# Mask copies ahead of the expert weights, and the second expert weights in 112 and 6 rows

## The chip, the cores and the metric

The kernel runs on one core of a Trainium2 chip. The metric is the device time of one execution in microseconds. It computes two transformer blocks in float32 for 8 batch rows of 100 tokens of 512 channels, with 361 context tokens.

## The reference

What is computed, cut to its outline (layer norms, softmax and quantisations are written out in full in the reference):

```
x = x + state_mix(layernorm(x), ctx)          # linear recurrence over ctx, its mean added, norm
x = x + bitlinear_ffn(layernorm(x))           # 512 -> 2048 -> 512, ternary weights, gelu
q = w8a8(layernorm(x), wq); k = ctx @ wk.T + bk; v = ctx @ wv.T + bv
s = q @ k.T / sqrt(32) + mask                 # 16 heads, mask of 100 x 361 per batch row
x = x + w8a8(softmax(s) @ v, wo)
g, e = top2(layernorm(x) @ gate.T + bias)     # 8 experts
x = x + sum(g * (silu(z @ w1[e].T + b1[e]) @ w2[e].T + b2[e]))
```

## The kernel before

The kernel is written engine by engine, with semaphores between them. There are three stages.

Stage A (to about 295 us) makes keys into `CT` (one slice per batch row) and values into `VS` (read as `vs(b)`) for all 8 batch rows, and runs the first attention and the feed-forward layer.

Stage B (from about 296 us, its loop from 340 us) is the attention, one batch row b at a time, 16 heads in 4 groups. TensorE (PE) makes the scores of a group, four heads at once (`scores`, L786), and runs one group ahead: the first scores of batch b + 1 are made within batch b. VectorE (DVE) adds the mask, takes the row minimum and writes `sN` (L1164, reading `maskS`), ScalarE takes the exponential (L598), PE turns the probabilities (L794) and multiplies them by the values (L807, `mix_group`). Between heads DVE also prepares the rows of batch b + 1 and finishes those of batch b - 1; GpSimd scales the queries that the next batch's first scores need. Having passed all heads of batch b, DVE makes a small copy (L1172) that raises `mask_used`.

`maskS` has two slots, and batch b uses slot b % 2. The masks of batches 0 and 1 are loaded in front of the loop (L310). The mask of batch b + 2 may be loaded once batch b is through, and DVE waits for it (`mask_in0`, `mask_in1`) when batch b + 2 begins.

SyncE (SP) issues all copies of this stage in program order, in `expert_loads(b, j, more)` (L313 to 320). When all scores of batch b are made, the keys of batch b are used up, and the first weights of expert b go into their place (L315, 704 KB, 128 rows). When all of batch b is mixed (semaphore `mixed`), its values are used up too, and the second weights of expert b go there (L317, 708 KB, 118 rows of 1536 floats). After it stands the wait for `mask_used` and the mask copy (L320, 141 KB, 100 rows of 361 floats). Batches 6 and 7 have `more` false, thus no mask to load.

Stage C (from about 556 us) routes the tokens to the experts. SP loads the router's weights and biases (L329 to L331, 16, 3.1 and 3.1 KB) and `b1B`, the first biases of all experts spread to 128 rows (L332, 1408 KB), and DVE waits for these four before its first instruction of the stage (L1191). PE waits for `experts_in`, the count of all expert copies, 16 for each copy. From 629 us on, 20 blocks of 128 rows run through the experts, bound by PE.

Of the kernel before, what the change touches and what calls it, by code (L numbers as in the profile page):

```python
# [14 lines left out]
B, S, D = 8, 100, 512  # L15
T = 361
# [11 lines left out]
WP = D * FF // P // NW  # L28
E, EH = 8, 352
EC = 118  # L30
EHP = 3 * EC
TOPK = 2
NBLK = (B * S * TOPK + E * (P - 1)) // P
# [7 lines left out]
def block_kernel(nc, x, ctxT, mask, decay, win, b_in, wout, b_out, gamma0, beta0, w1, w2, gammaf,  # L41
                 wq, bq, wk, bk, wv, bv, wo, bo, gate_w, gate_b, gate_bias, ew1, eb1, ew2, out):
    with ExitStack() as whole:  # L43
        def sb(stack, name, shape, dt=F32):
            return stack.enter_context(nc.sbuf_tensor(name, shape, dt))
# [3 lines left out]
        def sem(name):  # L49
            if name not in sems:  # L50
                sems[name] = whole.enter_context(nc.semaphore(name))
            return sems[name]
# [8 lines left out]
        def after(count):  # L61

            return count + 1
# [20 lines left out]
        def vs(b):  # L84
            return VS[:, bass.ds(b * (NT * VW), NT * VW)]
# [43 lines left out]
        maskS = sb(bb, "maskS", [P, 2, T + 1])  # L129
# [46 lines left out]
        share, backI = sb(cc, "share", [P, NBLK]), sb(cc, "backI", [P, NBLK], I32)  # L176
        hb, hs, hTe = sb(cc, "hb", [P, 2, EH]), sb(cc, "hs", [P, 2, EHP]), sb(cc, "hTe", [P, 2, 3, P])
        yb = sb(cc, "yb", [P, 2, D])
# [56 lines left out]
        def groups_mixed(groups):  # L235

            return groups + 2
# [7 lines left out]
        def read_by_heads(eng, b):  # L245

            for r in range(HPC):
                eng.wait_ge(sem(f"score{r}"), after((b + 1) * KC))
# [11 lines left out]
        def _(sp):  # L260
# [50 lines left out]

            def expert_loads(b, j, more):

                read_by_heads(sp, b)
                sp.dma_start(CT[:, b, 0:KC * EH], ew1[b]).then_inc(sem("experts_in"), 16)  # L315
                sp.wait_ge(sem("mixed"), groups_mixed((b + 1) * KC))
                sp.dma_start(vs(b)[0:EC, 0:3 * D], ew2[b]).then_inc(sem("experts_in"), 16)  # L317
                if more:
                    sp.wait_ge(sem("mask_used"), b + 1)
                    sp.dma_start(maskS[0:S, j, 0:T], mask[b + 2]).then_inc(sem(f"mask_in{j}"), 16)  # L320

            with sp.Fori(0, B // 2 - 1) as it:
                for j in range(2):
                    expert_loads(it * 2 + j, j, True)
            expert_loads(B - 2, 0, False)
            expert_loads(B - 1, 1, False)

            sp.wait_ge(sem("b_done"), 4)
# [24 lines left out]
        def _(g):  # L353
# [120 lines left out]
            for j in range(2):  # L474

                g.memset(hs[:, j, EH:EH + 1], 1.0).then_inc(sem("c_setup"), 1)
                g.memset(hs[:, j, EH + 1:EHP], 0.0).then_inc(sem("c_setup"), 1)
            g.iota(z[0:S, :, C_TOK:ZW], [[S, B], [0, ZW - C_TOK]], base=1, channel_multiplier=1,
# [25 lines left out]
        def _(act):  # L504
# [128 lines left out]
            def step(s, j, u):  # L633
                if started(s):
                    act.wait_ge(sem("h_turned"), s)
                    act.copy(hTe[0:EC, 1 - j].rearrange("p c s -> p (c s)"), ps[0:EC, 5 - j, 0:3 * P])\  # L636
                       .then_inc(sem("hT"), 1)
# [16 lines left out]
        def _(pe):  # L654
# [202 lines left out]
            pe.matmul(ps[:, 0, 0:1], ones[:, :], ones[:, 0:1], start=True, stop=True).then_inc(sem("b_done"), 1)  # L857

            pe.wait_ge(sem("b_done"), 4)
            pe.wait_ge(sem("experts_in"), 32 * E)  # L860
            pe.wait_ge(sem("c_in"), 64)

            for b in range(B + 1):
# [30 lines left out]
            def step(s, j, u):  # L894
# [7 lines left out]
                if started(s):  # L902
                    pe.wait_ge(sem("h_act"), s)
                    for c in range(3):
                        mm = pe.transpose(ps[0:EC, 5 - j, c * P:(c + 1) * P], hs[:, 1 - j, c * EC:(c + 1) * EC], ident[:, :])  # L905
                    mm.then_inc(sem("h_turned"), 1)
                if within(s, 1):
                    turn_x(s + 1, 1 - j, u + j)
                if started(s):
                    e = block_expert(mybir.EngineType.PE, s - 1)  # L910
                    pe.wait_ge(sem("hT"), s)
                    for c in range(3):
                        mm = pe.matmul(ps[:, 7 - j, :], hTe[0:EC, 1 - j, c, :], vs(e)[0:EC, c * D:(c + 1) * D],  # L913
                                       start=(c == 0), stop=(c == 2))
# [422 lines left out]
```

## Time and profile before

| | |
|---|---|
| runs | 773.19, 777.51, 779.58 us; median 777.51 |
| profiled execution | 778.72 us, its span 776.6 us |
| PE busy | 542.8 us, 70% |
| DVE busy | 365.1 us, 47% |
| ScalarE (ACT) busy | 296.9 us, 38% |
| GpSimd (POOL) busy | 179.6 us, 23% |
| DVE in stage B, waiting for scores | 51.0 us, 26 times |
| DVE in stage B, waiting for a mask | 18.8 us, 5 times |
| copies | 62.58 MB, mean 81 GB/s |

How to read it: the span is the time from the first to the last instruction in the profile; the execution's own time is 2.1 us more. A share of busy time is a mean over all stages. PEclk is the clock granted to TensorE as a part of 2.4 GHz; a full 1.00 or a 0.50 (1.2 GHz) stand in most short windows. The DMA share is the mean busy share of the core's 16 copy engines, so that two engines at work show as 0.12 or 0.13.

### The profile page before, as it was taken

The numbers are of one execution on the slowest core, as the hardware profiler recorded it, in microseconds if no ns is written. First come the engines' busy times: TensorE is split into PE (matmuls) and PEld (weight loads), VectorE is DVE, ScalarE is ACT, GpSimd is POOL, SyncE is SP. The second block draws the span as 40 slices with busy tenths as digits, with TensorE's granted clock in tenths as the row PEclk, the third lists the DMA queues.
The fourth block names the chain that finished last, engine by engine and source line by source line (L and its number), as shares of the span: only waits on it lengthen the run. The fifth ranks groups of instructions, "written<-read, shape, count | busy, mean of one in ns | idle before, by whom it ended". The sixth has DMA issues, their size and how long they took to land. (4 is left out here: it accounts for less than half of the span.)

```text
span 776.6 us, 10875 instructions
## 1 busy us (share of the span) xinstructions
PE 542.8 (70%) x3388; PEld 382.2 (49%) x3388; DVE 365.1 (47%) x962; ACT 296.9 (38%) x631; POOL 179.6 (23%) x211
## 2 busy tenths in 40 slices
PE   0062299999999993149967887769237049999991
PEld 0042277777777772126645655547137025555550
DVE  5646656676657663443655566644152112222210
ACT  4156333444343420435755666666011002222220
POOL 1001121332223220121323233421200611222221
PEclk9995589999999997555867688885655559999996
DMA  8959200000000003101212221212220434445544
GB/s 336 418 189 342 89 11 0 11 11 11 0 11 11 0 1 129 26 0 39 74 37 62 79 78 38 65 69 76 102 96 1 124 92 83 83 83 85 91 58 111
DMA packets 22915, 62.58 MB, mean 81 GB/s; under 512 B 3779, under 2 KB 9699, under 8 KB 20827
## 3 DMA queue, kind: packets, MB, share of 16 engines
q1 hardware_dynamic: 18462, 53.47, 20.1%
q0 software_dynamic: 4416, 8.63, 7.0%
q8 instruction: 22, 0.36, 0.2%
q14 instruction: 15, 0.11, 0.1%
HBM read 46.40 MB, written 17.32 MB: 82 GB/s over the span
## 5 line engine op out<-in xcount | busy, mean ns | idle before, releaser
L1164 DVE CUSTOM_DVE_ANT_0 sN<-ps,maskS 100x361 f32<-100x361 f32 x128 | 64.7, 532 | 79.8 <-PE ps L786 51.0
L794 PE MATMUL ps<-ident,pE 100*121 100x100 f32 x384 | 81.3, 349 | 8.1 <-ACT pT L589 8.0
L794 PEld LDWEIGHTS ps<-ident,pE 100*121 100x121 f32 x384 | 64.3, 241 | 43.3 <-issue 33.2
L598 ACT ACTIVATE pE<-sN,nmx 100x361 f32<-100x361 f32 x128 | 77.4, 605 | 21.2 <-DVE nmx L1164 21.2
L589 ACT COPY pT<-ps 121x300 f32<-121x300 f32 x128 | 51.3, 402 | 37.9 <-PE ps L794 37.8
L786 PE MATMUL ps<-CT,qn 32*100 32x361 f32 x256 | 39.9, 704 | 30.7 <-DVE nmx L1164 27.3
L913 PE MATMUL ps<-VS,hTe 118*128 x120 | 56.7, 609 | 5.5 <-ACT hTe L636 5.5
L499 POOL DMA_INDIRECT sums_out<-yb,backI x20 | 31.1, 1554 | 109.5 <-ACT yb L646 105.4
L899 PE MATMUL ps<-CT,xT 128*128 x160 | 53.3, 477 | 2.0 <-DVE xT L1257 2.0
L1271 DVE TENSOR_TENSOR hb<-ps,b1B 128x352 f32<-128x352 f32 x20 | 10.5, 525 | 88.7 <-PE ps L899 88.7
L899 PEld LDWEIGHTS ps<-CT,xT 128*128 128x128 f32 x160 | 31.3, 197 | 24.9 <-issue 12.8
L1046 DVE TENSOR_REDUCE tk<-h 100x1 f32<-100x512 f32 x32 | 20.0, 680 | 39.5 <-ACT h L549 39.4
L689 PE MATMUL ps<-cxH,wkH 128*128 128x364 f32 x128 | 31.1, 368 | 8.9 <-DVE cxL L984 4.5
L913 PEld LDWEIGHTS ps<-VS,hTe 118*128 118x128 f32 x120 | 21.1, 189 | 29.3 <-issue 29.3
L669 PE MATMUL ps<-kvw,w1s 128*128 128x8 f32 x32 | 7.0, 361 | 40.0 <-DMA y<-in_b_out 40.0
L891 PE MATMUL ps<-ident,xin 128*128 128x128 f32 x80 | 12.5, 281 | 30.2 <-DMA xin<-slots_in 30.2
L646 ACT ACTIVATE yb<-ps,share 128x512 f32<-128x512 f32 x20 | 13.7, 687 | 51.3 <-PE ps L913 51.3
L402 POOL TENSOR_SCALAR hq<-h 100x1024 bf16<-100x1024 f32 x8 | 10.3, 1290 | 93.8 <-DVE h L1053 93.8
L542 ACT ACTIVATE CT<-ps,biases 128x364 f32 (+1 forms) x32 | 17.9, 564 | 36.7 <-PE ps L689 35.8
L807 PE MATMUL ps<-pT,VS 121*32 121x100 f32 x768 | 30.5, 308 | 0.6 <-ACT pT L589 0.6
L786 PEld LDWEIGHTS ps<-CT,qn 32*100 32x100 f32 x256 | 11.6, 216 | 38.2 <-issue 31.1
L689 PEld LDWEIGHTS ps<-cxH,wkH 128*128 128x128 f32 x128 | 22.8, 206 | 14.3 <-issue 7.1
(233 smaller groups left out, 1141.7 us busy)
## 6 DMA issues: line engine op xcount, KB each, us to landing
VS<-in_w SPq DMA_DIRECT2D x8, 1024.0 KB, 9.2
CT<-in_ctxT SPq DMA_DIRECT2D x8, 728.0 KB, 16.8
VS<-in_ew SPq DMA_DIRECT2D x8, 708.0 KB
CT<-in_ew SPq DMA_DIRECT2D x8, 704.0 KB
slots_in<-zeros SPq DMA_DIRECT2D x5, 1056.0 KB, 12.4
xin<-slots_in SPq DMA_DIRECT2D x20, 264.0 KB, 3.4
XR<-in_x SPq DMA_DIRECT2D x1, 1600.0 KB
summB<-summary_rows SPq DMA_DIRECT2D x8, 200.0 KB
```

What stands on the lines that cost most here:

```text
L499: g.indirect_dma_start(sums_out, bass.IndirectOffsetOnAxis(backI[:, t:t + 1], 0), yb[:, t % 2, :], None, bounds_check=B * S + P - 1, compu ...
L542: act.activation(CT[:, b, m * TP:(m + 1) * TP], ps[:, m % 2, 0:TP], ACT.Identity, bias=biases[:, 1, m:m + 1]).then_inc(sem("k_copied"), 1)
L589: act.copy(pT[0:TC, ht % (2 * HPC)].rearrange("p c s -> p (c s)"), ps[0:TC, 4 + r, 0:NT * S])\
L598: act.activation(pE[0:S, q, 0:T], sN[0:S, q, 0:T], ACT.Exp, scale=-1.0, bias=nmx[0:S, h_:h_ + 1], accum_out=sums[0:S, j, h_:h_ + 1]).then_ ...
L689: mm = pe.matmul(ps[:, m % 2, 0:TP], wt[:, k, m * P:(m + 1) * P], cx[:, k, :], start=(n == 0), stop=(n == 3 * KC - 1))
L786: pe.matmul(ps[0:S, r, 0:T], qn[at, b % 2, g, :], CT[at, b, g * TP:g * TP + T], start=True, stop=True)\
L794: mm = pe.transpose(ps[0:TC, 4 + r, c * S:(c + 1) * S], pE[0:S, h_ % HPC, c * TC:(c + 1) * TC], ident[0:S, 0:S])
L807: mm = pe.matmul(ps[r * HD:(r + 1) * HD, 6, g * S:(g + 1) * S], vs(b)[0:TC, at:at + HD], pT[0:TC, (g * HPC + r) % (2 * HPC), c, :], start= ...
L899: mm = pe.matmul(ps[:, 2 + j, 0:EH], xT[:, j, k, :], CT[:, e, k * EH:(k + 1) * EH], start=(k == 0), stop=(k == KC - 1))
L913: mm = pe.matmul(ps[:, 7 - j, :], hTe[0:EC, 1 - j, c, :], vs(e)[0:EC, c * D:(c + 1) * D], start=(c == 0), stop=(c == 2))
L1046: ins = dve.tensor_reduce(tk[0:S, 14 + m:15 + m], h[0:S, m * 512:(m + 1) * 512], AX.X, ALU.max, apply_absolute_value=True)
L1164: dve.tensor_tensor_reduce(out=sN[0:S, q, 0:T], in0=ps[0:S, q, 0:T], in1=maskS[0:S, j, 0:T], scale=-1.0, scalar=3.4e38, op0=ALU.add, op1=A ...
```

## The change

The wait for `mask_used` and the mask copy go from the end of `expert_loads` to its beginning, ahead of the wait for the scores. The second weights go as two copies of 112 rows (`EVEN`, the largest multiple of 16 in 118) and 6 rows. Each raises `experts_in` by 16, so PE's wait at the start of stage C asks for 48 instead of 32 for each expert.

```diff
--- before.py
+++ after.py
@@ -28,6 +28,7 @@
 WP = D * FF // P // NW
 E, EH = 8, 352
 EC = 118
+EVEN = EC // 16 * 16
 EHP = 3 * EC
 TOPK = 2
 NBLK = (B * S * TOPK + E * (P - 1)) // P
@@ -311,13 +312,14 @@
 
             def expert_loads(b, j, more):
 
+                if more:
+                    sp.wait_ge(sem("mask_used"), b + 1)
+                    sp.dma_start(maskS[0:S, j, 0:T], mask[b + 2]).then_inc(sem(f"mask_in{j}"), 16)
                 read_by_heads(sp, b)
                 sp.dma_start(CT[:, b, 0:KC * EH], ew1[b]).then_inc(sem("experts_in"), 16)
                 sp.wait_ge(sem("mixed"), groups_mixed((b + 1) * KC))
-                sp.dma_start(vs(b)[0:EC, 0:3 * D], ew2[b]).then_inc(sem("experts_in"), 16)
-                if more:
-                    sp.wait_ge(sem("mask_used"), b + 1)
-                    sp.dma_start(maskS[0:S, j, 0:T], mask[b + 2]).then_inc(sem(f"mask_in{j}"), 16)
+                for rows in (slice(0, EVEN), slice(EVEN, EC)):
+                    sp.dma_start(vs(b)[rows, 0:3 * D], ew2[b, rows]).then_inc(sem("experts_in"), 16)
 
             with sp.Fori(0, B // 2 - 1) as it:
                 for j in range(2):
@@ -857,7 +859,7 @@
             pe.matmul(ps[:, 0, 0:1], ones[:, :], ones[:, 0:1], start=True, stop=True).then_inc(sem("b_done"), 1)
 
             pe.wait_ge(sem("b_done"), 4)
-            pe.wait_ge(sem("experts_in"), 32 * E)
+            pe.wait_ge(sem("experts_in"), 48 * E)
             pe.wait_ge(sem("c_in"), 64)
 
             for b in range(B + 1):
```

On SP, in the loop body of stage B, for one batch. Before, `CT<-in_ew` being the first and `VS<-in_ew` the second expert weights:

```order
L315 ISA [waits score2,score3,score1,score0]
L315 DMA CT<-in_ew 128x1408
L316 REGISTER_ALU
L317 ISA [waits mixed]
L317 DMA VS<-in_ew 118x1536
L320 ISA [waits mask_used]
L320 DMA maskS<-in_mask 100x361
```

and now (the row of L249 holds the wait for the scores):

```order
L317 ISA [waits mask_used]
L317 DMA maskS<-in_mask 100x361
L249 ISA
L319 ISA [waits score2,score3,score1,score0]
L319 DMA CT<-in_ew 128x1408
L320 REGISTER_ALU
L322 ISA [waits mixed]
L322 DMA VS<-in_ew 112x1536
L322 ISA
L322 DMA VS<-in_ew 6x1536
```

The mask copy has moved past both weights and both of their waits; the second weights are two copies.

On SP, from the last batch of B to the start of C. Before:

```order
L315 DMA CT<-in_ew 128x1408 [waits score2,score3,score1,score0]
L317 DMA VS<-in_ew 118x1536 [waits mixed]
L329 DMA gwT<-in_gate_w 128x32 [waits b_done]
L330 DMA gbB<-in_gate_b 100x8
L331 DMA gbB<-in_gate_bias 100x8
L332 DMA b1B<-in_eb 128x2816
```

and now:

```order
L319 DMA CT<-in_ew 128x1408 [waits score2,score3,score1,score0]
L322 DMA VS<-in_ew 112x1536 [waits mixed]
L322 DMA VS<-in_ew 6x1536
L331 DMA gwT<-in_gate_w 128x32 [waits b_done]
L332 DMA gbB<-in_gate_b 100x8
L333 DMA gbB<-in_gate_bias 100x8
L334 DMA b1B<-in_eb 128x2816
```

No mask stands here; only the second weights have become two copies, ahead of what stage C loads.

## Rows read from the trace of the kernel before

**Rows 1.** the page, part 1: busy time, share of the span, instructions

```profile
PE 542.8 (70%) x3388; PEld 382.2 (49%) x3388; DVE 365.1 (47%) x962; ACT 296.9 (38%) x631; POOL 179.6 (23%) x211
```

**Rows 2.** waits of DVE, 330 to 560 us: total, times, longest

```profile
DVE sN L1164 <- PE ps L786: 51.0, 26, 4.0
DVE sN L1164 <- DMA maskS<-in_mask: 18.8, 5, 5.0
```

**Rows 3.** timeline of DVE: start, us, line, tiles, [idle before <-releaser]

```profile
365.55 0.54 DVE L1164 CUSTOM_DVE_ANT_0 sN<-ps,maskS 100x361 f32<-100x361 f32 x1 [2.89 <-PE ps L786]
...
391.31 0.54 DVE L1164 CUSTOM_DVE_ANT_0 sN<-ps,maskS 100x361 f32<-100x361 f32 x1 [4.70 <-DMA maskS<-in_mask]
...
443.39 0.54 DVE L1164 CUSTOM_DVE_ANT_0 sN<-ps,maskS 100x361 f32<-100x361 f32 x1 [0.21 <-issue]
...
517.89 0.53 DVE L1164 CUSTOM_DVE_ANT_0 sN<-ps,maskS 100x361 f32<-100x361 f32 x1 [5.00 <-DMA maskS<-in_mask]
```

**Rows 4.** timeline of SP's copies, batch 0 to 1 of stage B

```profile
373.70 0.26 SPq L317 DMA_DIRECT2D VS<-in_ew  x1
374.17 0.29 SPq L320 DMA_DIRECT2D maskS<-in_mask  x1
```

**Rows 5.** windows of 1 us: length, busy time by engine, PEclk, DMA share, GB/s

```profile
384.00:385.00 1.00, 0.79 (x8) 0.53 (x6) 0.87 (x4) 0.85 (x2) 0.92 (x2) 1.00 0.98 393
388.00:389.00 1.00, 0.98 (x14) 0.79 (x6) 0.00 (x0) 0.48 (x3) 0.00 (x0) 1.00 0.12 49
392.00:393.00 1.00, 0.00 (x0) 0.00 (x0) 0.82 (x3) 0.95 (x3) 0.02 (x1) 0.54 0.03 8
```

**Rows 6.** windows of batches 0 to 7, first L1164 to L1172, columns as rows 5

```profile
340.59:362.51 21.92, 16.75 (x124) 11.72 (x125) 11.13 (x40) 11.62 (x37) 4.00 (x5) 0.50 0.06 16
365.55:386.47 20.92, 19.47 (x209) 13.85 (x208) 14.60 (x50) 15.54 (x50) 7.47 (x7) 0.77 0.19 64
391.31:413.95 22.64, 18.09 (x173) 12.28 (x173) 14.50 (x50) 14.45 (x46) 7.46 (x7) 0.70 0.21 64
417.68:443.04 25.36, 21.17 (x173) 14.59 (x173) 14.60 (x50) 14.44 (x46) 7.47 (x7) 0.60 0.20 63
443.39:465.14 21.75, 18.17 (x209) 12.63 (x207) 14.59 (x50) 15.71 (x52) 8.55 (x8) 0.84 0.23 70
467.21:488.74 21.53, 17.14 (x177) 11.38 (x176) 14.59 (x50) 14.33 (x46) 7.47 (x7) 0.84 0.22 67
492.49:512.75 20.26, 15.70 (x173) 10.76 (x173) 14.58 (x49) 14.33 (x46) 7.47 (x7) 0.83 0.19 67
517.89:536.64 18.75, 16.39 (x131) 11.21 (x131) 10.47 (x39) 11.64 (x37) 1.26 (x1) 0.51 0.15 52
```

**Rows 7.** copies by kind: KB each, us from issue to landing

```profile
wst<-in_wq SPq DMA_DIRECT2D x1, 1024.0 KB, 4.8
wst<-in_wo SPq DMA_DIRECT2D x1, 1024.0 KB, 6.9
```

**Rows 8.** timeline of PE, scores (L786), and of DVE at 447.53

```profile
385.80 0.87 PE L786 MATMUL ps<-CT,qn 32*100 32x361 f32 x8
...
394.41 1.54 PE L786 MATMUL ps<-CT,qn 32*100 32x361 f32 x8 [5.26 <-DVE nmx L1164]
...
446.49 0.87 PE L786 MATMUL ps<-CT,qn 32*100 32x361 f32 x8 [0.87 <-DVE nmx L1164]
447.53 0.54 DVE L1164 CUSTOM_DVE_ANT_0 sN<-ps,maskS 100x361 f32<-100x361 f32 x1 [1.18 <-PE ps L786]
...
512.09 0.87 PE L786 MATMUL ps<-CT,qn 32*100 32x361 f32 x8
```

**Rows 9.** timeline, end of B and start of C, SP and DVE

```profile
544.72 0.25 SPq L317 DMA_DIRECT2D VS<-in_ew  x1
...
557.44 0.35 SPq L332 DMA_DIRECT2D b1B<-in_eb  x1
...
565.49 0.69 DVE L1191 BATCH_NORM_STATS2 st6c<-XR 100x6 f32<-100x512 f32 x1 [9.71 <-DMA b1B<-in_eb]
```

## The prediction

> **What bounds the kernel now.** First the page's own totals [rows 1]: in a span of 776.6 us no engine is full, PE being busy for 70%, so the time is a sum of stages, each with its own last wait. The changed copies are issued in stage B (attention, from 340 us) and read in B (masks) and in stage C (experts). So I read who VectorE (DVE) waited for in B, and at the start of C [rows 2]. In B most of its idle time (51.0 us) ends on the scores from TensorE (PE), but 18.8 us, in five pieces, end on the copy of a mask. C begins with 9.7 us that end on a copy [rows 9].
>
> Next, where these five stand. DVE ends a batch with a small copy (L1172) and begins the next with the first L1164. The idle time ahead of that one tells [rows 3]: batch 2 begins after 4.70 us idle, batch 7 after 5.00 us, both for the mask (batches 3, 5 and 6 lie between, with 3.59, 1.93 and 3.60 us, all of the same kind). Batch 4 begins after 0.21 us, for nothing that the profile shows, and batch 1, whose mask is one of the two loaded in front of the loop, after 2.89 us, for the scores.
>
> Then why the mask is late [rows 4]: SP issues the second expert weights at 373.70 and the mask right behind, at 374.17; the mask is used at 391.31. That is 17.1 us for 141 KB. The windows say what the copy engines did in between [rows 5]: a share of 0.12 to 0.13 of 16 engines, or two engines, moving 49 GB/s, up to the moment the mask is in (392 to 393 us: 0.03). The first expert weights (704 KB) by contrast reach 0.98 and 393 GB/s. A 708 KB copy (725,000 bytes) at 50 GB/s takes 14.5 us, and what shares its two engines waits for it. So 118 rows go over two engines, and the mask's rows, whatever engines they are given, partly stand behind them.
>
> The Trainium skill, DMA: Bandwidth & Descriptors, section on why a DMA increments its semaphore by 16, says the number of engines is the largest up to 16 that divides the outer size of both sides: 118 gives 2, 112 gives 16, 6 gives 6, 100 gives 10. The share of 0.12 agrees for 118. The same page's rules for kernel authors speak against the second edit: two copies to disjoint partitions serialize on the same engines, so one should be used; by that the split is worth nothing and the sum below ends 1.5 us higher. The rule is written of copies that already use all 16, and the 0.12 of this trace is not that case.
>
> **The change part by part.** *Mask ahead of the weights (6 masks, batches 2 to 7).* Mask b+2 is now issued when batch b has ended: for batch 2 at 362.7 us instead of 374.17 (batch 0's window ends with its L1172 at 362.51 [rows 6]). It is needed at about 386.8. No such mask was seen travelling alone; the nearest row is a seven times larger copy that landed 4.8 us after issue [rows 7], and the farthest bound is the 17.1 us of today behind a slow copy. With either the mask is in by 380 us, 7 us before its need. All five stalls should go by this edit alone.
>
> What is late next at a batch's start: DVE's own L1172 and the scores. PE begins the scores of batch 2 at 385.80 and of batch 7 at 512.09, in both cases just before DVE is through [rows 8]; the three batches between are alike. From such a start at full clock to the first L1164 is 1.04 us (446.49 to 447.53). So batch 2 could begin at 386.84, 0.23 us after L1172's end (386.61, where its idle time of 4.70 begins), and batch 7 at 513.13, 0.24 us after. Batch 4 shows the same 0.21. Gain: 18.8 - 5 x 0.24 = 17.6 us. Bounds from the rows: all of it, 18.8; or, if each new batch waits for scores as batch 1 did at half clock (2.89 us), 4.70 + 3.59 + 3.60 + 5.00 - 4 x 2.89 = 5.3 us (batch 5 then gains nothing). I take 17.6, since these scores ran at full clock (0.87 us at 385.80 and at 512.09, against 1.54 us at 394.41, at half).
>
> Is the stall paid back within the batch? Batches 1 and 4 started without one and took 20.92 and 21.75 us; 2, 3, 5 and 6 started with one and took 22.64, 25.36, 21.53 and 20.26 [rows 6]. The starved ones are no faster, so nothing is given back.
>
> *The order on SP.* The wait for mask_used now stands ahead of the first expert weights, which so far went out at the batch's last scores. They are now issued when the batch has ended; nothing reads them before C, and the wait for "mixed" behind them opens later still (batch 0 ends at 362.51, its second weights go out at 373.70). Cost: 0. Batches 6 and 7 carry no mask and are not moved. The three queued items behind the new wait (weights 1, weights 2, next mask) serve nobody within this time.
>
> *112 and 6 rows.* Eight more copies of some 0.25 us on SP (the length of the old issue), which is idle: 0. For masks the split is cover, not gain. It pays at the end of B. The last second weights go out at 544.72 and, at 50 GB/s, hold two engines until about 560; b1B, the last copy that DVE needs for C, goes out at 557.44, and DVE starts C at 565.49 [rows 9]. With 16 engines the weights are in by about 549.5 (a copy of 1024 KB landed after 4.8 us), and b1B meets free engines. Bounds of the gain. From above: two 1024 KB copies issued 0.4 us apart landed 4.8 and 6.9 us after issue [rows 7], so a further 1024 KB costs 2.5 us; 1408 KB then need 2.3 + 3.5 = 5.8 us, landing at 563.3: gain 2.2 us. From below: by the bytes the old weights are done at 544.72 + 14.5 = 559.2 or soon after, and 14 of the 16 engines are free for b1B anyway, so memory may be its limit: 0. I take 1.5 us, nearer to the rows of whole copies, which are of the same kind.
>
> *The clock.* A stall of DVE becomes one of PE: behind batch 2's stall PE began the next scores at 394.41 after 5.26 us idle [rows 8], and the granted clock fell in 392 to 393 us (mean 0.54 of 2.4 GHz, thus mostly at the 1.2 GHz level) after 1.00 [rows 5]. By its windows [rows 6], a batch costs 25.36 us at a mean clock of 0.60 and (21.75 + 21.53 + 20.26) / 3 = 21.2 at 0.84: 4.16 / 0.24 = 17 us per whole unit of clock, or 104 us over batches 1 to 6. They average 0.76 today. Without stalls they may stand nearer to 0.84, worth up to 5.4 + about 3 in batch 7 (0.51). But batch 0 had no stall and ran at 0.50 throughout, so an unbroken batch is no promise. I take 2.5 us, with -10 and +10 as ends (a mean clock moved by 0.1 either way).
>
> The Trainium skill, TensorE: Matmul & The Clock Gate, Part 1, has it that an idle array falls to half rate and a busy one rises again; the fall behind the stall agrees, batch 0 does not bear out the rise. Applied in full, the rule gives rival 2 below.
>
> **Sum**, on the profiled execution (span 776.6, with 2.1 around it, 778.7): 778.7 - 17.6 - 1.5 - 2.5 = 757.1. That execution lies 1.2 us above the median of 777.51, so for a median: **756 us**, 2.8% less. A change of under 1% can hardly be told from none here (the three runs span 773.19 to 779.58).
>
> **Rivals.** *1. The scores take the mask's place.* If PE stands at half clock at the batch starts, each costs 2.89 us as batch 1's did, and the masks bring only 5.3 us. For it: batches 0 and 7 ran at half clock, and 51.0 us of DVE's idle time end on scores anyway. Against it: batch 4. Time: 777.5 - 5.3 - 1.5 = 770.7.
>
> *2. The clock stays up.* With no gap at any batch start the mean clock of batches 1 to 6 rises from 0.76 to about 0.90: 0.14 x 104 = 14.6 us on top of 19.1. Time: 777.5 - 33.7 = 743.8. For it: the falls behind the stalls. Against it: batch 4 itself averaged 0.84, so falls come also without a stall.
>
> *3. The clock stays down: slower.* The chip treats all of B as it did batch 0. Then six batches cost 25.4 us each, 19.9 more than today's 132.5, against 5.3 + 1.5 gained: 777.5 + 13.1 = 790.6. It decides against the change from the point where the mean clock of batches 1 to 6 falls by 19.1 / 104 = 0.18, to 0.58. For it: 21.9 us at 0.50 in batch 0. Against it: every later batch but the last rose of itself, the stalled ones too.
>
> *4. The masks stay late.* If the 17.1 us were due to something else than the two busy engines (the mask's own layout, say), starting it 11 us earlier need not help, and only the gain at C is left: 777.5 - 1.5 = 776. Only the window shares speak, and they speak against it.
>
> **Chances.** Forecast (750 to 765) 0.67; rival 1 0.13; rival 2 0.12; rival 3 0.03; rival 4 0.03; the rest for sizes between. Faster by over 1% (below 769.7): forecast, rival 2 and under half of rival 1 with what lies between, 0.88. Within 1%: 0.09. Slower by over 1%: 0.03. The range for 8 in 10 is the forecast's own, widened toward both near rivals, each of which it cuts short: 746 to 768.
>
> **What would show it.** In the profile after: no DVE idle on maskS at all; batches 2 to 7 beginning under 0.5 us after L1172 (about 2.9 would be rival 1); mask issues some 0.2 us after each L1172; no stretch of 0.12 share, and a burst like that of the first weights in its place; DVE's first bn_stats of C 6 to 7 us after b1B's issue instead of 8; batch lengths of 20 to 22 us with a mean clock near 0.84. The prediction is wrong if a mask wait is left, if the five starts are taken over by another wait of over 2 us, or if the summed batch lengths grow by more than 10 us.

## The result, and the profile after

The changed kernel takes 756.23 us (median of 4 runs, 753.36 to 771.10); the kernel before takes 775.42 us (median of 4, the three runs shown above and one more beside the changed kernel, 773.33 us). The ratio is 0.974 with a 95% interval of 0.969 to 0.979. The time of 756 us that was predicted is met, in the range of 746 to 768 us. The ratios here and below leave out runs more than 1.5% above the fastest of their kernel (here that of 771.10 us); medians and ranges are of all runs.

The page of the changed kernel, its span and part 1. The profiled execution took 753.36 us, the fastest of the four, 25 us less than the profiled one of before.

```profile
span 751.4 us, 10898 instructions
PE 528.9 (70%) x3388; PEld 371.9 (49%) x3388; DVE 365.3 (49%) x962; ACT 295.9 (39%) x631; POOL 179.6 (24%) x211
```

The waits of DVE from 330 to 560 us (total, times, longest), to be laid beside [rows 2]:

```profile
DVE sN L1166 <- PE ps L788: 48.1, 31, 4.0
DVE y L1156 <- PE ps L777: 11.4, 8, 3.1
DVE st6c L1193 <- DMA b1B<-in_eb: 8.3, 1, 8.3
```

The row of the mask is gone: in 128 uses of `maskS` DVE did not wait for a copy once. Its wait for the scores is hardly smaller (48.1 us for 51.0). The third row is the start of stage C.

The timeline of DVE at the start of batches 1, 2, 4 and 7, answering to [rows 3]:

```profile
364.95 0.54 DVE L1166 CUSTOM_DVE_ANT_0 sN<-ps,maskS 100x361 f32<-100x361 f32 x1 [2.89 <-PE ps L788]
...
386.34 0.53 DVE L1166 CUSTOM_DVE_ANT_0 sN<-ps,maskS 100x361 f32<-100x361 f32 x1 [0.32 <-PE ps L788]
...
431.45 0.54 DVE L1166 CUSTOM_DVE_ANT_0 sN<-ps,maskS 100x361 f32<-100x361 f32 x1 [0.31 <-PE ps L788]
...
498.56 0.54 DVE L1166 CUSTOM_DVE_ANT_0 sN<-ps,maskS 100x361 f32<-100x361 f32 x1
```

Batches 2 to 7 now begin after 0.32 us idle or less (batches 3, 5 and 6 are like 2 and 4), and where the profile names a releaser it is the scores. Batch 1 waits 2.89 us for its scores, to the hundredth what it did before. How to read such a row: the number in the bracket is the stall, the name behind it says what to look at next.

SP's copies for batch 0, answering to [rows 4]; the mask first, then the second weights as two copies:

```profile
362.25 0.30 SPq L317 DMA_DIRECT2D maskS<-in_mask  x1
...
373.11 0.83 SPq L322 DMA_DIRECT2D VS<-in_ew  x2
```

and the windows of 1 us behind the latter, answering to [rows 5] (length, busy time by engine, PEclk, DMA share, GB/s):

```profile
374.00:375.00 1.00, 1.00 (x10) 0.63 (x8) 0.81 (x6) 1.00 (x5) 0.00 (x0) 0.74 1.04 203
375.00:376.00 1.00, 1.00 (x11) 0.47 (x11) 0.63 (x1) 1.00 (x5) 0.29 (x1) 1.00 0.90 344
376.00:377.00 1.00, 1.00 (x21) 0.83 (x24) 0.98 (x4) 0.98 (x4) 0.98 (x1) 1.00 0.45 148
377.00:378.00 1.00, 1.00 (x27) 0.74 (x19) 0.93 (x5) 0.26 (x1) 0.00 (x0) 1.00 0.08 31
```

The second weights are in within 5 us of their issue, at a share of up to 1.04 (in effect all 16) and 344 GB/s, where two engines were busy at 49 GB/s before.

Batches 1 to 7, first L1166 to L1174, answering to [rows 6]:

```profile
364.95:385.88 20.93, 19.48 (x209) 13.88 (x208) 14.58 (x50) 15.54 (x50) 7.46 (x7) 0.77 0.20 66
386.34:409.64 23.30, 19.76 (x209) 13.48 (x207) 14.58 (x50) 15.60 (x51) 8.43 (x8) 0.78 0.23 70
409.99:431.00 21.01, 17.11 (x209) 11.66 (x207) 14.59 (x50) 15.71 (x52) 8.55 (x8) 0.92 0.27 76
431.45:450.89 19.44, 15.53 (x209) 10.70 (x207) 14.57 (x49) 15.61 (x51) 8.47 (x8) 1.00 0.29 84
451.34:474.57 23.23, 19.69 (x209) 13.42 (x207) 14.58 (x49) 15.61 (x51) 8.45 (x8) 0.78 0.24 70
474.98:498.31 23.33, 19.79 (x209) 13.52 (x207) 14.59 (x50) 15.66 (x52) 8.49 (x8) 0.78 0.33 100
498.56:517.65 19.09, 16.26 (x183) 11.02 (x182) 11.32 (x40) 15.10 (x51) 3.74 (x3) 0.91 0.25 77
```

and, since the last window of [rows 6] ends with the last mask and not with the copy behind it, batch 7 of the kernel before up to that copy:

```profile
517.89:541.07 23.18, 20.82 (x149) 14.74 (x150) 11.14 (x41) 14.59 (x47) 1.26 (x1) 0.51 0.19 63
```

The start of stage C, answering to [rows 9]:

```profile
521.40 0.70 SPq L322 DMA_DIRECT2D VS<-in_ew  x2
...
534.13 0.35 SPq L334 DMA_DIRECT2D b1B<-in_eb  x1
...
540.78 0.69 DVE L1193 BATCH_NORM_STATS2 st6c<-XR 100x6 f32<-100x512 f32 x1 [8.32 <-DMA b1B<-in_eb]
```

From b1B's issue to DVE's first instruction it is 6.65 us now and was 8.05.

With the starts of such rows the whole difference of the two spans can be laid out (a gap is from the start of the copy that ends a batch to the first mask row of the next):

| stretch | before | after | less |
|---|---|---|---|
| to the first mask row of batch 0 | 340.59 | 339.99 | 0.6 |
| seven gaps between L1172/L1174 and the next batch | 22.92 | 5.41 | 17.5 |
| batch 0 | 21.92 | 21.92 | 0 |
| batches 1 to 6 | 132.46 | 131.24 | 1.2 |
| batch 7, to its last copy | 23.18 | 19.09 | 4.1 |
| from there to b1B's issue | 16.37 | 16.48 | -0.1 |
| b1B's issue to DVE's first instruction | 8.05 | 6.65 | 1.4 |
| stage C from there on | 211.11 | 210.62 | 0.5 |
| span | 776.6 | 751.4 | 25.2 |

This is one execution of each kernel. The changed kernel was profiled once more (its execution took 765.62 us), and there the batches came out otherwise. The stretch from the first mask row of batch 1 to the copy that ends batch 6, in the kernel before, in this execution and in the second one:

```profile
365.55:512.75 147.20, 120.17 (x1254) 83.42 (x1253) 88.16 (x299) 96.42 (x305) 51.20 (x47) 0.78 0.20 64
364.95:498.31 133.36, 113.49 (x1254) 78.33 (x1253) 88.21 (x300) 95.84 (x305) 51.17 (x47) 0.84 0.26 77
363.97:508.88 144.91, 126.27 (x1254) 87.65 (x1253) 88.26 (x299) 96.47 (x306) 51.17 (x47) 0.74 0.24 70
```

All three hold the same 1254 matmuls. In the second execution the mask waits are gone too and the seven gaps add up to 5.94 us, but the stretch is only 2.3 us shorter than before, at a mean clock of 0.74: its batches 1 to 6 took 142.93 us, 10.5 us more than before.

### The profile page after: what moved, and what is told of

Same layout as the page of the kernel before. It is cut to its first block and busy times, and to the rows that moved or that the text cites. A ratio compares the mean times of both kernels' runs of the same rounds, so it can differ in the third digit from the quotient of the medians.

```text
span 751.4 us, 10898 instructions
## 1 busy us (share of the span) xinstructions
PE 528.9 (70%) x3388; PEld 371.9 (49%) x3388; DVE 365.3 (49%) x962; ACT 295.9 (39%) x631; POOL 179.6 (24%) x211
## 5 line engine op out<-in xcount | busy, mean ns | idle before, releaser
L1166 DVE CUSTOM_DVE_ANT_0 sN<-ps,maskS 100x361 f32<-100x361 f32 x128 | 64.4, 532 | 58.1 <-PE ps L788 48.1
L796 PE MATMUL ps<-ident,pE 100*121 100x100 f32 x384 | 75.2, 327 | 9.7 <-ACT pT L591 9.4
L796 PEld LDWEIGHTS ps<-ident,pE 100*121 100x121 f32 x384 | 58.7, 221 | 42.0 <-issue 29.2
L1273 DVE TENSOR_TENSOR hb<-ps,b1B 128x352 f32<-128x352 f32 x20 | 10.5, 524 | 88.8 <-PE ps L901 88.8
L788 PE MATMUL ps<-CT,qn 32*100 32x361 f32 x256 | 36.6, 649 | 19.5 <-DVE nmx L1166 16.2
L724 PE MATMUL ps<-w1s,xqT 128*100 128x512 fp8e4 x128 | 29.0, 379 | 0.0
L740 PE MATMUL ps<-w2s,hqT 128*100 128x512 fp8e4 x128 | 28.9, 379 | 0.0
```

What stands on the lines that cost most here:

```text
L724: mm = pe.matmul(ps[0:S, 2 + m, :], xqT[:, k, :], w1q[:, k * FF + m * 512:k * FF + (m + 1) * 512], start=(k == 0), stop=(k == KC - 1))
L740: mm = pe.matmul(ps[0:S, 7, :], hqT[:, k, :], w2q[:, k * D:(k + 1) * D], start=(k == 0), stop=(k == FC - 1))
L788: pe.matmul(ps[0:S, r, 0:T], qn[at, b % 2, g, :], CT[at, b, g * TP:g * TP + T], start=True, stop=True)\
L796: mm = pe.transpose(ps[0:TC, 4 + r, c * S:(c + 1) * S], pE[0:S, h_ % HPC, c * TC:(c + 1) * TC], ident[0:S, 0:S])
L1166: dve.tensor_tensor_reduce(out=sN[0:S, q, 0:T], in0=ps[0:S, q, 0:T], in1=maskS[0:S, j, 0:T], scale=-1.0, scalar=3.4e38, op0=ALU.add, op1=A ...
```

## The experiments

The theory was: the mask waits in its queue behind a copy that keeps two engines busy; each of the two edits frees it by itself; the start of C gains by the split alone. The rivals: that the split is what brings the masks in time, that the mask is late because SP issues it late, and that most of the gain is the clock.

**The changed kernel again.** No edit; this and the next two and the one on the start of C ran on one chip.

> The changed kernel itself, beside the three others on one chip. Expected: ratio 0.974 as measured, about 756 us; no DVE idle on maskS. If the gain in stage B were mostly luck of the granted clock, the ratio would scatter up to 0.99.

Measured: ratio 0.9731 (0.967 to 0.9793), median 759.01 us of 6 runs, from 748.62 to 765.62, while 11 runs of the kernel before lay between 772.13 and 779.1. The gain is there again, and every run of the one is below every run of the other. But the changed kernel scatters more widely. The runs line up with the mean clock of the execution: 748.62 us at 0.85, 758.51 at 0.829, 765.62 at 0.816.

**Only the first edit.** The diff is against the changed kernel, and PE's wait asks for 32 again.

```diff
-                for rows in (slice(0, EVEN), slice(EVEN, EC)):
-                    sp.dma_start(vs(b)[rows, 0:3 * D], ew2[b, rows]).then_inc(sem("experts_in"), 16)
+                sp.dma_start(vs(b)[0:EC, 0:3 * D], ew2[b]).then_inc(sem("experts_in"), 16)
```

> Only the first edit: masks issued ahead, second weights in one copy of 118 rows. Theory (the mask waits behind a copy that holds two engines; either edit alone frees it; the split adds only at the start of C): no DVE idle on maskS, stage B as in the changed kernel, DVE's wait at the start of C back from 6.65 to about 8.05 us after b1B's issue; time 1.4 us above the changed kernel, ratio 0.975. Rival (the split brings the masks in time): the five stalls stay, 775 us.

Measured: ratio 0.9777 (0.9731 to 0.9822), median 758.09 us, no wait for a mask. The timeline at the start of C (SP's second weights and b1B, and DVE):

```profile
517.74 0.25 SPq L321 DMA_DIRECT2D VS<-in_ew  x1
...
530.46 0.35 SPq L333 DMA_DIRECT2D b1B<-in_eb  x1
...
539.25 0.69 DVE L1192 BATCH_NORM_STATS2 st6c<-XR 100x6 f32<-100x512 f32 x1 [10.46 <-DMA b1B<-in_eb]
```

The wait behind b1B's issue is 8.79 us, even a little more than the 8.05 of before. The theory holds: the masks need only this edit, the start of C needs the other. The ratio is 0.005 above that of the changed kernel run beside it, but the two intervals overlap and the medians (758.09 and 759.01 us) stand the other way round: in whole times the two are not told apart.

**Only the second edit.** Against the kernel before; the masks stay behind the weights:

```diff
-                sp.dma_start(vs(b)[0:EC, 0:3 * D], ew2[b]).then_inc(sem("experts_in"), 16)
+                for rows in (slice(0, EVEN), slice(EVEN, EC)):
+                    sp.dma_start(vs(b)[rows, 0:3 * D], ew2[b, rows]).then_inc(sem("experts_in"), 16)
                 if more:
                     sp.wait_ge(sem("mask_used"), b + 1)
                     sp.dma_start(maskS[0:S, j, 0:T], mask[b + 2]).then_inc(sem(f"mask_in{j}"), 16)
```

> Only the second edit: 112 and 6 rows, masks still issued behind them. Theory: the second weights take some 4 us instead of 14.5, the mask lands about 4 to 6 us after its issue, some 8 us before its need, no DVE idle on maskS, time equal to the changed kernel (ratio 0.974). Rival (the mask is late because SP issues it late, behind two waits): stalls of 2 to 4 us stay at five batch starts, 765 to 775 us.

Measured: ratio 0.9716 (0.9667 to 0.9766), median 755.03 us. The timeline of SP for the mask of batch 2, and DVE's first use of it:

```profile
371.34 0.84 SPq L319 DMA_DIRECT2D VS<-in_ew  x2
372.38 0.30 SPq L322 DMA_DIRECT2D maskS<-in_mask  x1
...
389.21 0.53 DVE L1166 CUSTOM_DVE_ANT_0 sN<-ps,maskS 100x361 f32<-100x361 f32 x1 [0.21 <-issue]
```

The mask is issued 1.04 us behind the weights, nearly as late as before (372.38 against 374.17), and the batch begins 16.8 us later with 0.21 us idle. So the lateness of the issue alone did not make the stall. Either edit alone takes away all waits for a mask; together they don't add up, but for the start of C.

**The suspected cost doubled: 59 and 59 rows, in the order of before.** Against the kernel with only the second edit:

```diff
-EVEN = EC // 16 * 16
+EVEN = EC // 2
```

> The suspected cost doubled: order of before, second weights as two copies of 59 rows. Theory (the number of engines is the largest up to 16 that divides the rows, 59 gives 1, and both copies lie on the same engine): DMA share 0.06, 25 GB/s, 29 us for the second weights, the mask behind them; stalls of 12 us or more at each of the six starts of batches 2 to 7 and C starting 13 us later: 850 to 870 us. Rival (the copy is slow for another reason, such as its place in memory or its row length): as before, 775 us.

Measured: 882.66 us, ratio 1.1346 (1.1277 to 1.1414). DVE's waits for the mask, and a window of 1 us in the middle of one:

```profile
DVE sN L1166 <- DMA maskS<-in_mask: 85.7, 6, 17.5
```

```profile
390.00:391.00 1.00, 0.00 (x0) 0.00 (x0) 0.00 (x0) 0.00 (x0) 0.00 (x0) 1.00 0.06 25
```

A share of 0.06 is one engine, and 25 GB/s is half of what two moved. Six stalls of up to 17.5 us, where there were five of up to 5.0. The cause of the stalls is as expected; the time was 13 us over the expected 850 to 870. What the expectation had too small was the start of C: DVE waits 37.1 us there for b1B, 27.4 more than before, where 13 were expected. SP stood 10.53 us in the issues of the last second weights (from 623.20) and 13.22 us in that of gwT, and b1B went out behind them, at 651.51. The Trainium skill, DMA: Bandwidth & Descriptors, section on why a DMA increments its semaphore by 16, has the rule of the largest divisor up to 16, which gives one engine for 59 rows and two for 118; the shares of 0.06 and of 0.12 agree.

**The same slow copies, masks ahead.** The kernel changed as under study, with `EVEN = EC // 2`.

> The same slow weights with the masks ahead. Theory: weights of batch b - 1 are issued 5 us into batch b and done 29 us later, 13 us into batch b + 1; the mask of batch b + 2, issued at the end of batch b, lands behind them, 7 us before its need: no DVE idle on maskS, stage B as in the changed kernel; but C starts 13 to 15 us later, behind the last weights: 769 to 771 us. Rival (a copy issued ahead overtakes what is on the engine, or order does not matter at all): B with stalls as in the run beside it, 850 us.

Measured: 835.11 us, ratio 1.0734 (1.067 to 1.0799); the expectation missed by 65 us. The waits for the mask:

```profile
DVE sN L1166 <- DMA maskS<-in_mask: 23.2, 3, 9.0
```

and SP's second weights of batches 0, 2 and 7, then what follows them, gwT and b1B (start, length of the issue):

```profile
373.07 0.69 SPq L322 DMA_DIRECT2D VS<-in_ew  x2
...
419.15 12.57 SPq L322 DMA_DIRECT2D VS<-in_ew  x2
...
557.30 26.67 SPq L322 DMA_DIRECT2D VS<-in_ew  x2
...
584.02 14.19 SPq L331 DMA_DIRECT2D gwT<-in_gate_w  x1
...
601.75 0.35 SPq L334 DMA_DIRECT2D b1B<-in_eb  x1
```

Three stalls came, of 5.42, 8.87 and 8.96 us, at batches 5, 6 and 7, and none at 2, 3 and 4. The expectation took each batch's weights as starting when they are issued. But one engine needs about 29 us (725,000 bytes at 25 GB/s) for what is issued every 22 to 29 us, and the mask comes on top, so each batch adds to a backlog, and a mask put in behind it is later each time. From batch 1 on SP itself no longer gets rid of its copies: issuing two of them took 0.69 us for batch 0, 4.42 us for batch 1, 12.57 us for batch 2 and 26.67 us for batch 7, and gwT's took 14.19 us. b1B went out at 601.75, 44 us later than in the kernel before; DVE began C at 621.63. A mask ahead of its own batch's weights still stands behind all earlier ones: the first edit protected batches 2 to 4, and no longer once the backlog had grown.

**The masks on another queue.** The kernel before, with the second weights in one copy of 118 rows and all masks issued by GpSimd (also the first two, not shown here).

```diff
+                if not first and not last:
+                    g.wait_ge(sem("mask_used"), b)
+                    g.dma_start(maskS[0:S, 1 - j, 0:T], mask[b + 1]).then_inc(sem(f"mask_in{1 - j}"), 16)
                 if not last:
                     scale_q(b + 1, 1 - j)
...
-                if more:
-                    sp.wait_ge(sem("mask_used"), b + 1)
-                    sp.dma_start(maskS[0:S, j, 0:T], mask[b + 2]).then_inc(sem(f"mask_in{j}"), 16)
```

> 118 rows in one copy as before, but the masks are issued by GpSimd, on its own queue, about 13 us into a batch, while the second weights of the batch before are still being copied on SP's queue. Theory of the queue (the mask waits in its queue's order, and copies of two queues share an engine): the mask lands within some 4 us, no or hardly any DVE idle on maskS, about 758 us. Rival (the busy engine serves whatever was issued first, whichever the queue): the mask lands with the end of the second weights, 20 to 25 us into the batch, stalls of 1 to 5 us stay, 765 to 775 us.

Measured: ratio 0.9704 (0.9644 to 0.9763), median 756.69 us, no wait for a mask. The issues of a pair, SP's weights and then GpSimd's mask; the six masks' time from issue to landing; and a window 12 us behind the mask's issue:

```profile
393.54 0.25 SPq L314 DMA_DIRECT2D VS<-in_ew  x1
...
398.60 0.66 POOL L448 DMA_DIRECT2D maskS<-in_mask  x1
```

```profile
DMA to landing us min/median/max: 5.6/6.3/6.7
```

```profile
410.00:412.00 2.00, 1.13 (x12) 0.60 (x11) 0.82 (x5) 1.71 (x6) 1.76 (x2) 1.00 0.13 53
```

Issued 5.1 us behind the weights, the mask is in at about 405 us, while two engines are still at work at 410 to 412 us (share 0.13). What held the mask was thus the order of its queue, not the engines being busy: the copy from another queue got its turn beside the slow one.

**The wait at the start of C.** On top of the change, b1B gets a semaphore of its own:

```diff
-            sp.dma_start(b1B[:], eb1.partition_broadcast(P)).then_inc(sem("c_in"), 16)
+            sp.dma_start(b1B[:], eb1.partition_broadcast(P)).then_inc(sem("b1_in"), 16)
...
             dve.wait_ge(sem("b_done"), 4)
-            dve.wait_ge(sem("c_in"), 64)
             dve.wait_ge(sem("c_setup"), 8)
...
             dve.wait_ge(sem("logit"), B)
+            dve.wait_ge(sem("c_in"), 48)
...
             dve.wait_ge(sem("block_experts"), 1)
+            dve.wait_ge(sem("b1_in"), 16)
```

(PE's wait asks for 48 instead of 64.)

> The changed kernel, and b1B has a semaphore of its own, for which DVE waits only ahead of the expert blocks; DVE's and PE's wait for the other three copies stands where gwT and gbB are first read. Theory: the wait at the start of C (8.3 us idle of DVE, of which 6.65 behind b1B's issue) is on the path and falls to under 3 us (setup of GpSimd): 5 to 7 us faster than the changed kernel, about 750 us, ratio 0.966. Rival: the wait for GpSimd's setup, for x_kept or for the indirect copies takes its place and nothing is gained.

Measured: ratio 0.9651 (0.9599 to 0.9703), median 750.79 us of 6 runs, against 0.9731 for the changed kernel on the same chip: 0.008, or 6.2 us. DVE's first instruction of C:

```profile
540.03 0.69 DVE L1192 BATCH_NORM_STATS2 st6c<-XR 100x6 f32<-100x512 f32 x1 [1.62 <-POOL part L482]
```

It waits 1.62 us, for GpSimd's setup, instead of 8.32 us for a copy; nothing else took its place. It has the lowest ratio of the study, clear of the kernel before; against the changed kernel the two intervals still overlap a little (0.967 to 0.9703), and the 6.7 us less idle in the trace is the firmer evidence.

**A stall of known length put back.** On top of the change, at the start of batches 1 to 7, n = 3 and n = 6:

```diff
+                if not first:
+                    for k in range(n):
+                        dve.tensor_reduce(hold[0:S, k:k + 1], bvB[0:S], AX.X, ALU.max, apply_absolute_value=True)
```

> The price of a stall by itself: the changed kernel, with three maximum-reductions of 0.68 us each on VectorE at the start of batches 1 to 7, into a tile of their own that nobody reads (about 2.0 us each time, 14 us in all). Theory (a stall is paid nearly in full): +12 to +15 us over the changed kernel, about 770. Rival (ends of the batch before are done meanwhile and given back, some 1 to 1.5 us a stall): +4 to +8 us, about 762.

> The same with six reductions (about 4.1 us each time, 28.7 us in all; the mask stalls of before were 18.8 in five). Theory: +27 to +32 us, with a lower mean clock as well: 783 to 790. Rival with giving back: +18 to +23 us, 775 to 780. The clock: if idle PE at the batch start is what lowers it, the mean granted clock of stage B falls below 0.75 as before; if not, it stays at 0.80.

Measured: with n = 3 ratio 0.9957 (0.9896 to 1.0018), with n = 6 ratio 1.0004 (0.9951 to 1.0056), 10 runs each. The six together held DVE for 3.64 us, less than the 4.1 expected:

```profile
384.78 3.64 DVE L1165 TENSOR_REDUCE hold<-bvB 100x1 f32<-100x512 f32 x6
```

So the three held it for some 1.9 us (estimated as half). (Batch 1's lay partly beside the wait for its scores.) The changed kernel was not run beside these two; over its earlier 0.974 the cost is 0.0217, or 16.8 us, for 13 us of holding, and 0.0264, or 20.4 us, for 25 us, each uncertain by about 6 us when the intervals are put together. With n = 3 that fits the theory (12 to 15) and not the rival (4 to 8), with n = 6 the rival (18 to 23) and not the theory (27 to 32); neither holds for both. That the second dose cost less than the first is not shown either: the two ratios are 0.0047 apart, within their intervals, and the medians of all ten runs are 775.69 and 775.42 us. A window of n = 6, batch 5:

```profile
472.82:493.10 20.28, 15.73 (x173) 10.80 (x173) 14.58 (x51) 14.35 (x46) 7.47 (x7) 0.83 0.19 57
```

It counts 173 matmuls of PE in 20.28 us at a clock of 0.83. The unheld batches 1 to 6 of the changed kernel count 209. The difference of 36 is the end of the batch before, done while DVE was held. The kernel before shows the same in the stall ahead of its batch 2, where PE works off 40 matmuls with DVE idle:

```profile
386.47:391.31 4.84, 2.67 (x40) 2.00 (x36) 0.14 (x3) 1.82 (x6) 1.28 (x1) 1.00 0.13 52
```

That is the giving back. With n = 3 batches 2 to 6 count 205, 203, 179, 205 and 179: the shorter hold let less be done ahead. In the profiled executions the mean clock of stage B's batches 1 to 6 was 0.73 with n = 6 and 0.61 with n = 3. The expectation's sign for the clock (below 0.75 if idle at the batch start lowers it) decides nothing, since the changed kernel without any hold also stood at 0.74 in its second trace. Whole executions of n = 3 averaged from 0.773 to 0.832 and took from 788.28 down to 762.55 us. Why the shorter hold ran at the lower clock was not found, and its cost can't be told from the clock's.

## Why the prediction was right, and where it was off

**The cause of the stall: right, and shown.** Two engines for 118 rows: the share halves with 59 rows and becomes full with 112. The mask behind them in its queue: on another queue it lands in 6.3 us while they still run. The Trainium skill, DMA: Bandwidth & Descriptors, rules for kernel authors, advises against splitting a copy by partitions, because both halves use all 16 engines anyway. That was not so here (0.12), and the split alone gave 0.9716; the prediction saw that the condition was missing.

**The masks' 17.6 us: right.** The gaps fell by 17.5 us. The working by the next limiter (L1172 and the scores at full clock, 0.24 us) was met at 0.1 to 0.32 us. Rival 1 did not come about: the scores ahead of these six starts took 0.87 us, as at full clock in [rows 8]. The prediction put this gain down to the first edit alone and called the split "cover, not gain" for the masks. It is more than that, since it frees the masks by itself.

**The new order on SP and eight more copies, 0: right.** The first weights went out 0.7 to 1.2 us behind each mask, and no engine waits for SP's issues in stage B.

**The start of C, 1.5 us: right**, 1.4 us in the trace. Its cause, the split, is shown by leaving it out (8.79 us), though in the whole times that is inside the intervals. The idle time of DVE there tells it too: 8.27 to 8.34 us in the five traces with the split and b1B in its old place, 9.71 to 10.46 in the three with one copy of 118 rows.

**"The starved ones are no faster, so nothing is given back": wrong.** This step put the give-back at nothing. It compared lengths without regard to the clock, and overlooked what [rows 6] already showed in their brackets: a starved batch counts 173 matmuls, an unstarved one 209. The stalled batches had 36 matmuls fewer to wait for. At like clock the unstarved are mostly longer: 23.23 to 23.33 us at 0.78 in three batches of the changed kernel, against 21.79 at 0.77 in a batch that followed a stall of 5.42 us (59 and 59 rows, masks ahead), thus 1.5 us. In [rows 6], at 0.83 to 0.84, it is 0.2 and 1.5 us (21.75 us against 21.53 and 20.26). Batch 1, with 209 matmuls in 20.92 us at 0.77, does not fit, so the size is rough. The window of the batch after the stall:

```profile
465.98:487.77 21.79, 16.81 (x173) 11.14 (x173) 14.58 (x50) 14.33 (x46) 7.47 (x7) 0.77 0.19 64
```

**The clock, 2.5 us: its size is not borne out; that the sum was met is in part luck.** In the first trace the mean clock of batches 1 to 6 rose from 0.76 to 0.84, as the prediction thought it might. At its slope of 104 us per unit that would be 7.8 us; the six batches got 1.2 us shorter. The 6.6 us between are of the size of what was given back (four of the six had been stalled), so here two errors nearly cancelled. The slope itself stands: the unstarved batches alone give (23.3 - 19.44) / 0.22 = 17.5 us per unit, or 105 us for six. For batch 7 the prediction had "about 3", from a window that ended too early; it fell by 4.1 us, at a clock of 0.91 instead of 0.51. All batches together brought 5.3 us in this execution. In the second trace the clock of batches 1 to 6 was 0.74, below that of before, and they were 10.5 us longer, just past the 10 us that the prediction named as a sign of being wrong. By the medians the whole gain is 19.2 us, and 15.3 in the repeat, while the gaps and the start of C make 18.9, so clock and give-back together come to about nothing or a small loss. What of the clock is owed to the change is not settled.

**Rivals 2 and 3**: the clock neither stayed up nor stayed down. The lowest and the highest of the changed kernel's ten runs are 748.62 and 771.10 us; none reached rival 2's 743.8 or rival 3's 790.6. The slowest lies at rival 1's 770.7, but not for rival 1's reason as far as the traces show: in both, no start of batches 2 to 7 waits more than 0.8 us.

## What to carry to other kernels

Look at the DMA share behind a copy, not only at its size: a steady 0.12 or 0.06 means one or two engines at work, and the number of rows on the outermost side is the first suspect. What a small urgent copy waits for is the queue that it stands in, so put it ahead, or on another queue, or make what is before it short; here one of these sufficed, as long as no backlog grew. And when a stall is removed, count the instructions in a stalled and an unstalled stretch before its whole length is entered as gain: work that ran during the stall comes back.

## What the runs showed of the hardware that was not expected

An issue of a copy on SP took 0.25 to 0.6 us as long as the queue was short, and up to 27 us (two copies) where one engine had a backlog of several copies; everything behind it on SP waited as well.

The granted clock fell within batches that had no gap at their start. Batch 2 of the changed kernel ran at a mean of 0.78, batch 4 at 1.00, both with 209 matmuls and 0.32 or 0.31 us idle ahead of them; the same pairs of length and clock (19.44 us at 1.00, 21.0 at 0.92, 23.3 at 0.78) came back in other kernels of the study. Both have a gap of PE of 1.12 us in their middle, yet the scores behind it ran at half clock in batch 2 and at full clock in batch 4:

```profile
395.00 1.54 PE L788 MATMUL ps<-CT,qn 32*100 32x361 f32 x8 [1.12 <-DVE nmx L1166]
...
440.12 0.87 PE L788 MATMUL ps<-CT,qn 32*100 32x361 f32 x8 [1.12 <-DVE nmx L1166]
```

The clock was 1.00 in the 9 us ahead of the one (from 386 us) and, after it, 0.50 until about 405 us. So a fall came behind this gap once and not the other time, with the same work on both sides of it; why is not shown.

Without the stalls the time of a run may be less steady: on the same chip the six runs of the changed kernel lie within 17 us against 7 us for eleven of the kernel before. But six runs with the first edit alone lie within 9.4 us, and on another chip 19 runs of the kernel before within 13.5 us, so this is not shown. An argument for it, not tested: a period that was tied to the arrival of the mask took up what the clock did in between.
